# Value projection of an adaptive-layernorm block: four half-size products and one VectorE operation become one full-size product and four VectorE operations

## The reference

```python
h = _layernorm(x) * (1 + ca) + sa
# attention, 16 heads of 8
qkv = (h @ Wqkv.T + bqkv).reshape(B, H, S, 3 * hd)      # a plain reshape, with no transpose
q, k, v = jnp.split(qkv, 3, axis=-1)
attn = softmax(einsum('bhsd,bhtd->bhst', q, k) / sqrt(hd))
x = x + ga * (einsum('bhst,bhtd->bhsd', attn, v).reshape(B, S, D) @ Wo.T + bo)
h = _layernorm(x) * (1 + cb) + sb
# router: softmax over 8 experts, the best 2, their weights and probabilities
x = x + gb * experts(h)
```

## Time and profile before

| | |
|---|---|
| time, 3 runs | 565.9 us median (565.25 to 566.61) |
| the profiled execution | 566.31 us |
| its span in the trace | 564.5 us |
| TensorE matmul busy | 521.4 us, 92% |
| ScalarE busy | 487.7 us, 86% |
| VectorE busy | 363.8 us, 64% |
| GpSimd busy | 223.2 us, 40% |
| mean granted TensorE clock | 0.981 |

### The profile page before, as it was taken

How to read it: one execution, slowest core, us unless ns; L and a number is a source line. 1 busy time by engine, 2 the same in 40 slices (tenths; PEclk the granted TensorE clock), 3 DMA queues, 4 the chain that set the end, 5 groups by cost and what they waited for, 6 DMA issues and landing times.

```text
span 564.5 us, 14303 instructions
## 1 busy us (share of the span) xinstructions
PE 521.4 (92%) x4046; PEld 215.1 (38%) x4046; DVE 363.8 (64%) x1276; ACT 487.7 (86%) x546; POOL 223.2 (40%) x436
## 2 busy tenths in 40 slices
PE   7489899999999999999999999999999999998753
PEld 6233333343443434333343433434343343333232
DVE  4435367666777676666677767666776776664464
ACT  1389999999999999999999999999999999999600
POOL 1222333444444433343444443334444444323337
PEclk9999999999999999999999999999999999999966
DMA  4473333333333333333233333333333333330100
GB/s 100 125 203 91 97 78 88 93 100 80 74 92 89 90 87 94 97 91 83 72 87 91 89 87 89 98 97 86 81 75 88 91 89 91 94 95 24 26 15 14
DMA packets 85496, 48.43 MB, mean 86 GB/s; under 512 B 61508, under 2 KB 76240, under 8 KB 85456
## 3 DMA queue, kind: packets, MB, share of 16 engines
q1 hardware_dynamic: 70468, 43.18, 30.1%
q10 hardware_dynamic: 14988, 4.72, 3.7%
HBM read 32.91 MB, written 14.94 MB: 85 GB/s over the span
## 4 chain that ended last, share of the span: by engine, by line
PE 82%; ACT 9%; DVE 3%; POOL 2%; issue 2%; DMA 1%; SPq 0%; ACTq 0%; POOLq 0%; DVEq 0%
PE ps_attn L677 42%; PE ps_scores L659 21%; ACT probs L523 9%; PE ps_side L707 8%; PE ps_side L597 4%; PE ps_side L604 2%; PE ps_side L613 1%; PE ps_side L690 1%; PE ps_side L591 1%; PE ps_side L694 1%; PE ps_side L584 1%; PE ps_scores L707 1%; DMA wqkv_in<-in_L_attn_Wqkv_dram 0%; POOL mix L459 0%; DVE weighted L1073 0%
## 5 line engine op out<-in xcount | busy, mean ns | idle before, releaser
L523 ACT ACTIVATE probs<-ps_scores 128x1024 f32<-128x1024 f32 x512 | 485.7, 1028 | 41.9 <-DMA q_scr<-qk_parts 19.7
L677 PE MATMUL ps_attn<-probs,values 128*32 128x512 f32 x2048 | 248.4, 599 | 0.2 <-issue 0.2
L659 PE MATMUL ps_scores<-query_stack,key_stack 32*128 32x512 f32 x1024 | 130.8, 500 | 16.5 <-ACT probs L523 10.9
L659 PEld LDWEIGHTS ps_scores<-query_stack,key_stack 32*128 32x128 f32 x1024 | 49.4, 183 | 166.9 <-ACT probs L523 162.2
L412 POOL TENSOR_SCALAR var_eps<-moments 128x1 f32<-128x1 f32 x64 | 12.2, 191 | 231.1 <-DVE moments L1004 158.9
L677 PEld LDWEIGHTS ps_attn<-probs,values 128*32 128x32 f32 x2048 | 54.1, 109 | 110.6 <-issue 110.6
L707 PE MATMUL ps_side<-experts_gated,h2T 128*128 (+1 forms) x228 | 74.7, 409 | 0.0
L993 DVE RECIPROCAL sums_inv<-sums 128x128 f32<-128x128 f32 x32 | 30.4, 951 | 33.6 <-DMA attnT<-a_scr 33.6
L1073 DVE TENSOR_TENSOR weighted<-ps_side,coef 128x256 f32<-128x256 f32 x114 | 46.5, 408 | 2.4 <-PE ps_side L707 2.4
L1000 DVE TENSOR_TENSOR x<-ps_side,x_gated 128x128 f32<-128x128 f32 x30 | 8.7, 292 | 59.8 <-PE ps_side L707 56.0
L459 POOL TENSOR_TENSOR mix<-weighted 128x512 f32<-128x512 f32 x32 | 40.9, 1278 | 0.0
(11 more groups left out here) (119 smaller groups left out, 507.3 us busy)
## 6 DMA issues: line engine op xcount, KB each, us to landing
key_stack<-k_scr SPq DMA_DIRECT2D x128, 128.0 KB, 2.7
query_stack<-q_scr SPq DMA_DIRECT2D x121, 64.0 KB, 2.3
q_scr<-qk_parts SPq DMA_DIRECT2D x188, 32.0 KB, 2.0
k_scr<-qk_parts SPq DMA_DIRECT2D x64, 64.0 KB, 1.7
a_scr<-attn ACTq DMA_DIRECT2D x124, 18.0 KB
sums<-a_scr SPq DMA_DIRECT2D x32, 64.0 KB, 2.2
attnT<-a_scr SPq DMA_DIRECT2D x32, 64.0 KB, 2.3
out_dram<-out_all ACTq DMA_DIRECT2D x28, 64.0 KB, 1.9
```

Of the source, the lines that this page charges most:

```text
L523: nc.scalar.activation(probs[:, k % RING, g, :], ps_scores[:, slot(k, g), :], ACT.Exp, scale=SCALE)\
L659: mm = nc.tensor.matmul(out_, key_stack[p0:p0 + 32, parity, 2 * k:2 * k + 2, :].rearrange("p j r -> p (j r)"), query_stack[p0:p0 + 32, par ...
L677: mm = nc.tensor.matmul(ps_attn[q:q + 32, :], values[:, parity, g, k, :], probs[:, k % RING, g, h * HALF:(h + 1) * HALF], start=(k == 0), ...
```

## The change

The value projection of a tile becomes one product: all 128 tokens of `hT` are stationary and all 128 columns of `wvT` move. Its result has tokens in partitions, both groups one under the other, and in columns first the 64 of the even column groups and then the 64 of the odd ones. Of the four quarters of 64 x 64, only those with g equal to odd have the partitions that `values` wants. VectorE now does four operations of 64 x 64, one for each quarter, that read rows 64 g and write rows 64 odd. The bias tile `bv` grows from 64 to 128 columns, so that each quarter finds its bias on the rows that it reads. Only the last of the four raises `values_done`.

```diff
-        bv = sb("bv", [P, KT, hd])
+        bv = sb("bv", [P, 2, KT, hd])
...
             def a_project_v(u1, ring, col):
 
-                for n in range(G):
-                    for odd in range(2):
-                        mm = nc.tensor.matmul(ps_side[odd * R:(odd + 1) * R, col + n * R:col + (n + 1) * R],
-                                              hT[:, ring, n * R:(n + 1) * R], wvT[:, odd].rearrange("p k d -> p (k d)"),
-                                              start=True, stop=True)
-                mm.then_inc(ev["v_ps_done"], 1)
+                nc.tensor.matmul(ps_side[:, col:col + P], hT[:, ring, :], wvT[:].rearrange("p o k d -> p (o k d)"),
+                                 start=True, stop=True).then_inc(ev["v_ps_done"], 1)
...
             def a_values(u1, ring, col):
                 reached(dve, ev["v_ps_done"], u1)
-                v.scalar_tensor_tensor(out=values[:, ring, :, :, 0:hd],
-                                       in0=ps_side[:, col:col + P].rearrange("p (g k d) -> p g k d", g=G, d=hd),
-                                       scalar=VALUE_SCALE, in1=spread(bv[:], 1, G), op0=ALU.mult, op1=ALU.add)\
-                    .then_inc(ev["values_done"], 1)
+                for g in range(G):
+                    for odd in range(2):
+                        rows, cols = slice(g * R, (g + 1) * R), slice(col + odd * R, col + (odd + 1) * R)
+                        ins = v.scalar_tensor_tensor(out=values[odd * R:(odd + 1) * R, ring, g, :, 0:hd],
+                                                     in0=ps_side[rows, cols].rearrange("p (k d) -> p k d", d=hd),
+                                                     scalar=VALUE_SCALE, in1=bv[rows, odd], op0=ALU.mult, op1=ALU.add)
+                ins.then_inc(ev["values_done"], 1)
...
                 for odd in range(2):
-                    ins = v.tensor_scalar(bv[odd * R:(odd + 1) * R], bq[odd * R:(odd + 1) * R, odd, :, 2, :], VALUE_SCALE, None, ALU.mult)
+                    ins = v.tensor_scalar(bv[:, odd], bq[:, odd, :, 2, :], VALUE_SCALE, None, ALU.mult)
```

## The result

The changed kernel takes 586.68 us (median of 6 runs, 585.63 to 587.59) against 566.12 us before (6 runs). The ratio is 1.0369, with a 95% interval of 1.0356 to 1.0381: 3.7% slower, 20.6 us. The forecast was 582.6 us in a range of 574.5 to 588.0.

What follows compares the result with a forecast made beforehand. Each loop tile was taken as bound by VectorE and GpSimd up to TensorE's norms product; 16.3 + 0.26 + 0.5 - 0.4 = 16.7 us on the profiled 566.31 gave 583.0, or 582.6 us from the median, range 574.5 to 588.

Steps and rivals of the forecast that it cites:

- The path: In each loop tile, VectorE's values through GpSimd's squares to TensorE's norms product; no slack, so 0.68 us is paid in full.
- The fork at the end of L677: TensorE product whose end splits each tile into TensorE's own branch and one through VectorE and GpSimd.
- the join at the norms product: TensorE's L613 at side 3, where both branches arrive within 0.05 us, the VectorE branch last.
- The size of the four quarters: VectorE's four operations take 0.88 us in place of 0.20, adding 0.68 us a tile, 16.3 us over 24 tiles.
- the hand-over: Gap between successive VectorE quarters on changing halves: 0.005 us, from two bias operations 0.19 us apart lasting 0.18.
- Held or overlapping: Whether VectorE's quarters wait for the one ahead, adding 0.68 us a tile, or overlap, adding 0.36; held was forecast.
- the rival of 574.7 us: VectorE's quarters overlap whatever half they work on, adding 0.36 us a tile; chance 0.12.
- The wait at side 2: TensorE's L597 waits some 0.45 us for the last quarter; free beside the norms product's wait, 7 us alone.
- The product: TensorE's value product shrinks from 0.38 to 0.25 us, a gain of 0.13 us a tile, worth nothing in the loop.
- that cover: TensorE's wait at L613, which hides the shorter product's 0.13 us in each of 24 loop tiles.
- Outside the loop: Prologue loses 0.5 us, tile 28 0.26 us, and the shorter product gives back 0.4 us in three other tiles.
- The clock: TensorE's granted clock was expected not to drop, though it would stand about 0.8 us more a tile.

Runs made afterwards that it cites:

- squares first: The changed kernel with GpSimd's squares put ahead of its two mix additions: 575.56 us, ratio 1.0155.
- the three cuts of the quarters: VectorE's four 64 x 64 operations with halves alternating, two by two, or all on the lower half: 585.97, 579.77 and 574.22 us.
- the alternating one: The kernel before, half-size products kept, VectorE's operation cut into four quarters, each within one half, ordered lower, upper, lower, upper: 585.97 us, ratio 1.0348.
- the two-by-two one: The kernel before, half-size products kept, VectorE's operation cut into four quarters ordered lower, lower, upper, upper half: 579.77 us, ratio 1.0243.
- the kernel on one half: The changed kernel with all four quarters reading and writing the lower 64 partitions, output wrong: 574.22 us, ratio 1.0139.
- Squares first in the kernel of before: The kernel before with GpSimd's squares put ahead of its two mix additions, nothing else: 565.24 us, ratio 0.9976.
- bank and squares first: GpSimd's squares ahead of its mix additions and VectorE's router top two behind the values: 569.71 us in the changed kernel, 566.78 us in the kernel before.

## Why the prediction was right, point by point

- **The path.** Right. The fork at the end of L677 and the join at the norms product bind every tile of the loop: the norms product stays 0.05 us behind squares, the three cuts of the quarters appear in the period one for one, and squares first takes away more than half of the loss.
- **The size of the four quarters.** The direction was right and the size 13% small: 0.68 us a tile forecast, 0.78 measured, 16.3 against 18.7 us over the loop. The term that was mis-sized is the hand-over, taken from the single pair of the earlier trace rows as 0.005 us: it is 0.01 to 0.03 us, so that the four quarters with their hand-overs take 0.95 us where 0.88 had been worked out. The duration was almost right (216 ns forecast, 219 on the mean). That is 0.07 of the missing 0.10 us. Of the rest, 0.01 us is `pair_w`, which starts 0.20 us behind `pair_inv` in place of 0.19, and 0.01 to 0.02 us is the stretch at the start of a pass, which comes with the full-size product; the quarters with half-size products don't have it, and show 0.76.
- **Held or overlapping.** Held. The Trainium skill's rule ("VectorE: DVE Perf Modes", section "Two Vector instructions with no wait between them") counts four held starts in the changed kernel and in the alternating one, two in the two-by-two one and none on one half. The three measured distances, 0.95, 0.75 and 0.53 us, are equal steps for it. Here the trace agrees, and the rival of 574.7 us, the quarters that overlap, is the kernel on one half, at 574.2 us.
- **The wait at side 2.** Foreseen at 0.45 us, measured 0.47 and 0.36 us in the two tiles of a pass. That it costs nothing beside the later one was right. What it would cost alone was forecast as 7 us; with squares first the loop is 7.4 us longer than before, and the whole run 9.4 us on the median, with the lower clock of two of its four runs in it.
- **The product.** Right that it is worth nothing here (567.34 us). Its length was forecast as 0.25 us and is 0.22. The step "were that cover gone it would be worth 3.1 us" was wrong: with the cover gone it gave nothing that can be measured. ScalarE's exponential takes back part of it, and the stretch at the start of a pass the rest; the prediction counted TensorE's own products as if nothing stood behind them.
- **Outside the loop.** The norms product of the prologue came 0.33 us late against 0.5 forecast, tile 28 0.38 against 0.26. The hole of 1.25 us in the first pass was not foreseen; that of 0.88 us at tile 2 went. All that lies outside the loop's period, holes included, comes to 20.4 - 18.7 = 1.7 us, where 0.36 was forecast; that the hole which went hides most of the new one is luck, not foresight.
- **The clock.** As forecast, no drop: 0.981 on the mean before, 0.982 after.

## What to carry to other kernels

An engine that is busy for two thirds of the time isn't free: before work is moved to it, find who waits for the operation behind it. A distance between two engines that is the same 0.05 us in every iteration is a path with no slack, and whatever is added ahead of it is paid in full in every iteration, while the time saved on the other branch is worth nothing. Where an operation has to be cut by partitions, order the pieces so that neighbours start on the same partitions, and count the operation that follows them too.

## What the runs showed of the hardware

A VectorE operation that starts on another half of the partitions than the one ahead costs 0.10 to 0.11 us more, with the same elements (0.95, 0.75 and 0.53 us for the same four operations). With it, cutting 128 x 128 into four 64 x 64 makes 0.95 us out of 0.20.

VectorE's second operation on `qk_parts`, which has two inputs in SBUF, isn't slowed by GpSimd but stopped by it: wherever a GpSimd operation was running when it started, in all versions, it ends 0.27 to 0.29 us after that one has ended. So it takes 0.71 us beside squares in the prologue, 0.91 in the loop before and after, 1.39 with squares first, beside GpSimd's first mix addition, and 2.48 beside an operation of 2.43 us. With no GpSimd operation beside it it takes 0.42 to 0.43 us. The cast ahead of it (L935) ends 0.15 to 0.16 us behind the GpSimd operation in the same way, and takes 0.29 to 0.30 us where none was running at its start. Squares first in the kernel of before changes GpSimd's list alone and moves it from 0.91 to 1.39 us. In the loop before, in the prologue before, and with bank and squares first:

```profile
258.02 0.74 POOL L461 TENSOR_TENSOR mix<-mix 128x256 f32<-128x256 f32 x1
258.13 0.91 DVE L937 TENSOR_TENSOR qk_parts<-qkT,qk_parts 128x256 fp32r<-128x256 f32 x1
```

```profile
10.53 0.72 POOL L420 TENSOR_TENSOR squares<-qkT 128x256 fp32r<-128x256 f32 x1 [5.49 <-DVE qkT L926]
10.81 0.71 DVE L937 TENSOR_TENSOR qk_parts<-qkT,qk_parts 128x256 fp32r<-128x256 f32 x1
```

```profile
274.67 1.33 POOL L459 TENSOR_TENSOR mix<-weighted 128x512 f32<-128x512 f32 x1
274.89 1.39 DVE L933 TENSOR_TENSOR qk_parts<-qkT,qk_parts 128x256 fp32r<-128x256 f32 x1
```

TensorE has holes of 0.4 to 1.25 us at places that move when instructions are added ahead of them, and with the full-size product a stretch of 0.02 to 0.32 us at the start of a pass of the loop. That both come from how its instructions are supplied is likely, but no run here shows it.
